# Block attention: scores on 32-row tiles of TensorE, values and softmax sums computed transposed on four column tiles, division there

## The reference, cut to what matters

```
b, s, d = x.shape                       # 16, 128, 128;  H = 16 heads, HD = 8
q, k, v = (split_heads(x @ W) for W in (Wq, Wk, Wv))
scores = einsum('bhqd,bhkd->bhqk', q, k) / sqrt(HD)
attn_w = softmax(scores, axis=-1)
ctx = einsum('bhqk,bhkd->bhqd', attn_w, v)      # back to [b, s, d]
attn_out = ctx @ Wo + bo
out1 = layernorm(x + attn_out, ln1_g, ln1_b)    # the experts read out1
```

## Time and profile before

| | |
|---|---|
| time, median of 3 runs | 1621.97 us (1621.96 to 1628.43) |
| the profiled execution's own time | 1623.44 us |
| its span | 1621.7 us |
| the stage at hand | about 1164 to 1349 us of the span |
| TensorE clock granted, mean | 0.92 of full |

### The profile page before, as it was taken

One profiled execution on the slowest core, in us unless ns is written; L12 is line 12 of the kernel. 1 busy time (PEld: TensorE's weight loads), 2 busy tenths in 40 slices (PEclk: granted clock), 3 DMA queues, 4 the chain that ended last, 5 costly groups with the idle time before them and its releaser, 6 DMA issues. The chain is left out here.

```text
span 1621.7 us, 27487 instructions
## 1 busy us (share of the span) xinstructions
PE 1397.8 (86%) x9061; PEld 1085.9 (67%) x9061; DVE 839.1 (52%) x2258; ACT 728.3 (45%) x1657; POOL 146.7 (9%) x256
## 2 busy tenths in 40 slices
PE   6765689999998789959999997995499996999995
PEld 5631367777777457749999995994377773667664
DVE  4548466666664445445454553345777772122224
ACT  4341466666664311225555553342255551433433
POOL 1010000000000000000000002004233430000000
PEclk9878699999999799969999997996599995999998
DMA  8000000000000000000000001202000000000000
GB/s 323 1 1 0 1 1 2 1 1 1 1 1 1 1 1 1 1 0 1 1 2 1 1 1 43 75 2 104 0 1 1 0 1 0 1 1 1 0 1 26
DMA packets 6429, 24.55 MB, mean 15 GB/s; under 512 B 797, under 2 KB 1311, under 8 KB 5418
## 3 DMA queue, kind: packets, MB, share of 16 engines
q1 hardware_dynamic: 6314, 23.03, 4.1%
HBM read 21.98 MB, written 1.05 MB: 14 GB/s over the span
## 5 line engine op out<-in xcount | busy, mean ns | idle before, releaser
L1304 DVE SCALAR_TENSOR_TENSOR XN<-bank,gate,XN 128x128 f32<-128x128 f32 x256 | 89.9, 351 | 224.7 <-PE bank L1268 222.2
L1284 ACT ACTIVATE e_hidden<-bank,small 128x512 f32<-128x512 f32 x152 | 104.4, 687 | 214.5 <-PE bank L1256 214.5
L765 PE MATMUL bank<-a_va,a_pT 128*128 128x65 f32 x1024 | 130.3, 270 | 0.7 <-ACT a_pT L931 0.6
L1009 DVE TENSOR_REDUCE a_mx<-bank 128x4 f32<-128x512 f32 x128 | 87.8, 686 | 80.2 <-PE bank L805 80.1
L1268 PEld LDWEIGHTS bank<-attention_weights,e_hidden 128*128 128x128 f32 x1024 | 119.2, 192 | 14.8 <-issue 14.8
L765 PEld LDWEIGHTS bank<-a_va,a_pT 128*128 128x128 f32 x1024 | 125.2, 193 | 2.4 <-ACT a_pT L931 1.1
L1256 PE MATMUL bank<-XNT,attention_weights 128*128 128x512 f32 x256 | 121.2, 606 | 1.3 <-PEq L541 1.3
L1268 PE MATMUL bank<-attention_weights,e_hidden 128*128 128x128 f32 x1024 | 119.3, 275 | 0.0
L830 PE MATMUL bank<-attention_weights,a_cv 128*128 128x256 f32 x256 | 84.4, 411 | 15.5 <-issue 15.5
L931 ACT ACTIVATE a_pT<-bank 128x512 f32<-128x512 f32 x128 | 76.1, 595 | 41.9 <-PE bank L839 39.2
L1017 DVE TENSOR_TENSOR a_shifted<-bank,a_mx 128x512 f32<-128x512 f32 x128 | 88.3, 690 | 3.4
(11 more groups left out here) (351 smaller groups left out, 2718.2 us busy)
## 6 DMA issues: line engine op xcount, KB each, us to landing
attention_weights<-in_a SPq DMA_DIRECT2D x2, 2048.0 KB, 11.6
mod_ring<-in_mod_weights SPq DMA_DIRECT2D x4, 576.0 KB
ctx_both<-in_ctx SPq DMA_DIRECT2D x1, 2048.0 KB, 10.1
attention_weights<-in_up SPq DMA_DIRECT2D x1, 2048.0 KB, 7.6
attention_weights<-in_down SPq DMA_DIRECT2D x1, 2048.0 KB, 13.2
down<-in_down SPq DMA_DIRECT2D x1, 1536.0 KB, 18.5
down<-in_mod_weights SPq DMA_DIRECT2D x2, 576.0 KB
X<-in_x SPq DMA_DIRECT2D x4, 256.0 KB, 3.5
```

The costliest lines, as they stand in the source:

```text
L765: last = pe.matmul(value_bank[:, j * (W + 1):(j + 1) * (W + 1)], pT[:, i.slot(2), j * 128:(j + 1) * 128], va[:, p, g // 2 * 8 + 2 * j + g ...
L1009: dve.tensor_reduce(mx[:, i.slot(2), :], score_bank[i.slot(2)][:, :].rearrange("p (h s) -> p h s", h=4), AX.X, ALU.max).then_inc(maxed, 1)
L1284: act.activation(hidden[0:rows, p, f, :], up_bank_of(i, f)[0:rows, :], function, bias=up_bias(g, f)).then_inc(hidden_ready, 1)
L1304: dve.scalar_tensor_tensor(out=total, in0=down_bank[j][:, e * D:(e + 1) * D], scalar=gate_column(k, 4 * q + j, g * per_group + e), in1=tot ...
```

## The change

**Scores.** GpSimd makes one spread block per batch instead of four: `own[row, j]` is 1 where the row's head is head j of its own group, so rows 32r to 32r+31 of `kD` hold the four heads of group r. The scores of group r are then a matmul over those 32 rows only. Two are issued together, in phases 3 and 1, into four score banks instead of two.

**Values.** They are computed transposed, once per batch: `va`, with each head's 8 columns 40 apart among zeros, is the stationary operand, 32 columns at a time; a head's `pT` streams, 128 columns, and the four heads of a group add up in PSUM (j = 0 to 3, each filling its 8 of 32 rows). Group c uses the column tile at 32c. The same with `ones` as the stationary operand gives each sum on the 8 rows of its head. So 32 matmuls of 128 columns stand where 16 of 9 columns did, and `pT` is kept for two whole batches.

**Division and behind it.** VectorE inverts 128 x 128 sums and multiplies once; the result is already `oT`. The transposition L1889 and the copy L1961 are gone. Of the normalisation's tail, VectorE keeps the first step; GpSimd does the two affine steps and the copy (`AFFINE`, a lag of 9 steps). The two side results share the projections' PSUM bank, hence new waits on `added` and `qkv_kept`; `KEEP` has moved behind the subtraction on VectorE, and `OUT` waits for it.

```
...
-    PROJECT, KEEP_QKV, BLOCKS, SCORE, EXP, TURN_P, VALUES, NORM_O, TURN_O, OUT, ADD, NORMALISE, KEEP, TURN_OUT = \
-        0, 1, 4, 3, 5, 5, 6, 6, 7, 7, 7, 8, 9, 10
+    PROJECT, KEEP_QKV, BLOCKS, SCORE, EXP, TURN_P, VALUES, NORM_O, OUT, ADD, NORMALISE, KEEP, TURN_OUT = \
+        0, 1, 2, 3, 5, 5, 6, 6, 7, 7, 8, 10, 10
+    AFFINE = 9
...
+        kD, va = sb("kD", [128, 2, 4, S]), sb("va", [128, 2, H * 40])
+        own, ones = sb("own", [128, 4]), sb("ones", [128, 4 * 40])
...
+        shifted, probs, pT = sb("shifted", [128, 2, 512]), sb("probs", [128, 2, 512]), sb("pT", [128, 2, 4, 512])
...
-        score_bank, turn_bank, value_bank = k.ps[0:2], k.ps[2:4], k.ps[4:6]
-        project_bank, side_bank = k.ps[6], k.ps[7]
...
+        score_bank, turn_bank, value_bank, project_bank = k.ps[0:4], k.ps[4:6], k.ps[6], k.ps[7]
+        turned_out = y_bank = project_bank[:, 384:512]
...
-            pool.memset(va[:, :, :, W:W + 1], 1.0).then_inc(cleared, 1)
+            pool.memset(va[:, :, :], 0.0).then_inc(cleared, 1)
+            pool.memset(ones[:, :], 0.0).then_inc(cleared, 1)
+            pool.wait_ge(cleared, 2)
+            pool.memset(ones[:, :].rearrange("p (j w) -> p j w", w=40)[:, :, 0:W], 1.0).then_inc(cleared, 1)
...
-                if i.alive:
-                    (b, g), p = i.part(4), (i.offset // 4) % 2
-                    await_count(pool, qkv_kept, b + 1)
...
-                    pool.tensor_tensor(kD[:, p, 4 * g:4 * g + 4, :], kT[:, p, :].unsqueeze(1).to_broadcast([128, 4, S]),
-                                       k.hmask[:, 4 * g:4 * g + 4].unsqueeze(2).to_broadcast([128, 4, S]),
-                                       ALU.mult).then_inc(k_spread, 1)
+                if i.alive and i.offset % 4 == 0:
+                    b = batch_of(i)
...
+                    await_count(pool, qkv_kept, n + 1)
...
+                    pool.tensor_tensor(kD[:, p, :, :], kT[:, p, :].unsqueeze(1).to_broadcast([128, 4, S]),
+                                       own[:, :].unsqueeze(2).to_broadcast([128, 4, S]), ALU.mult).then_inc(k_spread, 1)
+                i = at(AFFINE)
...
+                    await_count(pool, scaled_ready, n + 1)
...
+                    pool.tensor_tensor(out[:, p, :], scaled[:, p, :], k.affine3(2), ALU.mult).then_inc(chain, 1)
...
+                    pool.tensor_tensor(out[:, p, :], out[:, p, :], k.affine3(3), ALU.add).then_inc(out_ready, 1)
...
+                    pool.tensor_copy(col(k.out1, n), out[:, p, :]).then_inc(copied, 1)
...
+                    if b.older_than(3):
+                        await_count(pe, added, n - 2)
...
-                if i.alive:
+                if i.alive and i.offset % 2 == 0:
                     m, (b, g), p = i.number, i.part(4), (i.offset // 4) % 2
-                    await_count(pe, k_spread, m + 1)
...
-                        await_count(pe, subtracted, m - 1)
-                    pe.matmul(score_bank[i.slot(2)][:, :], qT[:, p, :],
-                              kD[:, p, 4 * g:4 * g + 4, :].rearrange("p h s -> p (h s)"), start=True,
-                              stop=True).then_inc(scored, 1)
-                i = at(TURN_O)
+                    await_count(pe, k_spread, b + 1)
+                    if i.older_than(4):
+                        await_count(pe, subtracted, m - 2)
+                    for r in (g, g + 1):
+                        rows = slice(32 * r, 32 * r + 32)
+                        pe.matmul(score_bank[r][:, :], qT[rows, p, :],
+                                  kD[rows, p, :, :].rearrange("p h s -> p (h s)"), start=True,
...
-                    await_count(pe, o_normed, b.number + 1)
+                    n, p = b.number, b.slot(2)
...
-                    pe.transpose(side_bank[:, 0:128], on[:, :], k.ident).then_inc(o_turned, 1)
-                i = at(VALUES)
-                if i.alive:
-                    m, (b, g), p = i.number, i.part(4), (i.offset // 4) % 2
...
-                        await_count(pe, o_normed, b - 1)
-                    for j in range(4):
-                        h = 4 * g + j
-                        last = pe.matmul(value_bank[p][:, h * (W + 1):(h + 1) * (W + 1)],
-                                         pT[:, i.slot(2), j * 128:(j + 1) * 128], va[:, p, h, :],
-                                         start=True, stop=True)
-                    last.then_inc(weighted, 1)
+                        await_count(pe, o_normed, n)
+                    else:
...
+                    for at_column, stationary, per_group in ((0, va[:, p, :], 160), (S, ones[:, :], 0)):
+                        for j in range(4):
+                            for c in range(4):
+                                first = c * per_group + 32 * j
+                                last = pe.matmul(value_bank[32 * c:32 * c + 32, at_column:at_column + S],
+                                                 stationary[:, first:first + 32], pT[:, p, c, j * 128:(j + 1) * 128],
+                                                 start=j == 0, stop=j == 3, tile_position=(0, 32 * c))
+                                if at_column and j == 3:
+                                    last.then_inc(weighted, 1)
...
-                    await_count(pe, o_kept, b.number + 1)
-                    pe.matmul(side_bank[:, 128:256], k.ones[0:1, :], k.bias3[0:1, :], start=True, stop=False)
...
+                    await_count(pe, o_normed, b.number + 1)
+                    if b.older_than(1):
+                        await_count(pe, out_kept, b.number)
+                    await_count(pe, qkv_kept, min(b.number + 3, B) if isinstance(b.number, int) else b.number + 3)
...
+                    b = batch_of(i)
+                    await_count(pe, out_ready, b.number + 1)
+                    await_count(pe, qkv_kept, min(b.number + 4, B) if isinstance(b.number, int) else b.number + 4)
+                    pe.transpose(turned_out, out[:, b.slot(2), :], k.ident).then_inc(out_turned, 1)
...
                     m, p = i.number, i.slot(2)
+                    (b, g), q = i.part(4), (i.offset // 4) % 2
                     await_count(act, p_turned, m + 1)
-                    if i.older_than(2):
-                        await_count(act, weighted, m - 1)
-                    act.activation(pT[:, p, :], turn_bank[p][:, :], ACT.Copy).then_inc(p_kept, 1)
+                    if i.older_than(8):
+                        await_count(act, weighted, 4 * b - 4)
+                    act.activation(pT[:, q, g, :], turn_bank[p][:, :], ACT.Copy).then_inc(p_kept, 1)
...
-                    dve.tensor_tensor(out[:, p, :], r1[:, :], k.affine3(3), ALU.add).then_inc(out_ready, 1)
...
-                    dve.tensor_scalar(col(k.out1, n), out[:, p, :], 1.0, None, ALU.mult).then_inc(chain, 1)
...
+                    dve.tensor_scalar(scaled[:, p, :], r1[:, :], stats[:, 6:7], stats[:, 7:8], ALU.subtract,
...
-                    dve.reciprocal(rec[:, :], o[:, :, W:W + 1].rearrange("p h w -> p (h w)")).then_inc(inverted, 1)
+                    dve.reciprocal(rec[:, :], value_bank[:, S:2 * S]).then_inc(inverted, 1)
...
-                        await_count(dve, o_turned, n)
-                    dve.tensor_tensor(on[:, :].rearrange("p (h w) -> p h w", h=H), o[:, :, 0:W],
-                                      rec[:, :].unsqueeze(2).to_broadcast([128, H, W]), ALU.mult).then_inc(o_normed, 1)
+                        await_count(dve, y_done, n)
+                    dve.tensor_tensor(oT[:, :], value_bank[:, 0:S], rec[:, :], ALU.mult).then_inc(o_normed, 1)
...
+                i = at(KEEP)
+                if i.alive and i.offset % 4 == 3:
+                    n = batch_of(i).number
+                    await_count(dve, out_turned, n + 1)
+                    dve.tensor_scalar(col(k.XNT, n), turned_out, 1.0, None, ALU.mult).then_inc(out_kept, 1)
```

More of the change, by code:

```diff
@@ L1857, in body @@
             def body(at):
-                i = at(TURN_OUT)
-                if i.alive and i.offset % 4 == 3:
-                    b = batch_of(i)
-                    await_count(pe, out_ready, b.number + 1)
-                    pe.transpose(side_bank[:, 256:384], out[:, b.slot(2), :], k.ident).then_inc(out_turned, 1)
                 i = at(PROJECT)
@@ L1914, in body @@
                     b = batch_of(i)
-                    await_count(pe, o_kept, b.number + 1)
-                    pe.matmul(side_bank[:, 128:256], k.ones[0:1, :], k.bias3[0:1, :], start=True, stop=False)
-                    pe.matmul(side_bank[:, 128:256], oT[:, :], k.w3[:, 384:512], start=False,
-                              stop=True).then_inc(y_done, 1)
+                    await_count(pe, o_normed, b.number + 1)
+                    if b.older_than(1):
+                        await_count(pe, out_kept, b.number)
+                    await_count(pe, qkv_kept, min(b.number + 3, B) if isinstance(b.number, int) else b.number + 3)
+                    pe.matmul(y_bank, k.ones[0:1, :], k.bias3[0:1, :], start=True, stop=False)
```

(27 more changed lines are left out.)

52 lines of the change are left out of this document (28 added, 24 removed).

## The result

The changed kernel takes 1646.33 us (median of 4 runs, 1639.37 to 1648.37), the kernel before 1621.97 (1617.24 to 1628.43, 4 runs): 1.0137 times, 95% interval 1.0115 to 1.0159. By the medians it is slower by 24 us. The profiled execution took 1645.0 us, against 1623.44.

What follows compares the result with a forecast made beforehand. TensorE bound the kernel before, a loop through all engines would bind after: 15 x (10.45 - 10.66) = -3 us, +3 for the ends, sum 0, so 1622 us relative to the median. Range 1608 to 1651; likeliest case 1612 to 1629.

Steps and rivals of the forecast that it cites:

- The loop through all engines: Block attention stage: waits tying all engines set the period, 10.40 us a batch, taken as 10.45, against 10.66; chance 0.56.
- the six legs: Parts of the loop, values round to values: 1.98, 2.00, 1.75, 1.66, 1.27 and 1.74 us, sum 10.40.
- Column tiles: Values matmuls on TensorE: four column tiles stream fully together, 1.72 us a batch; overlap only in part had chance 0.18.
- the rival at two together (+27): Values: only two column tiles stream together, +27 us, 1649; part of the 0.18 for column tiles in part.
- the mild one (+7): Values: four tiles stream together but lose a fifth, block 2.15 us, +7 us, 1629; chance 0.05.
- the changes of shape: TensorE passing between tile shapes: about 0.2 us each, seven a batch where two were, +1.0 us.
- VectorE: Inversion L2019 grows from 16 to 128 columns: 1.02 us, +0.76; VectorE's own chain 8.1 us a batch, not the bound.
- The ends: Start and end of the stage: +1.5 us for GpSimd's fills, the rest in the last batch; together +3 (0 to +5).
- the sum of 0 for the whole change: Whole kernel: 15 periods give -3 us, the ends +3, so 0; 1622 us relative to the median.
- The clock: Rival: TensorE, idle a quarter of the time, falls to 1.2 GHz; half the batches so +28 us, 1650; chance 0.10.
- the 0.9 that was named as a sign of being wrong: Profile sign: granted clock in the middle of the stage below 0.9 means the prediction is wrong; 1.00 was expected.
- a longer loop: The slower part of the loop case, over 0.5% slower than the kernel before; chance 0.10.

Runs made afterwards that it cites:

- e9: e1 with VectorE's inversion of 128 columns done twice, the first result unread; 1643.68 us.
- e8: e1 with the inversion cut from 128 columns to 16, the division by the other columns' sums left out; 1616.37 us.
- e2: The changed kernel with ScalarE's Ln and Exp of the moments one step later (NORMALISE 8 to 9); 1637.8 us.
- e1: The changed kernel with two useless f32 matmuls of 384 columns a batch on all 128 rows, in TensorE's waits; 1619.57 us.
- e5: e1 with the extra matmuls on 32 rows and 32 columns of TensorE; 1650.65 us.
- e10: e1 with the extra matmuls on all 128 rows and 32 columns of TensorE; 1622.52 us.
- e4: The changed kernel with the scores again as 128-row matmuls and GpSimd spreading k four times; 1649.78 us.
- e7: e3 with one of e1's extra matmuls a batch; 1608.92 us.
- e3: The changed kernel with the moments' Ln and Exp a step later and behind the pT copy, and ScalarE's Exp a step earlier; 1636.36 us.
- e11: e7 with five more matmuls of 512 columns behind the last values of the masked attention, the stage before; 1608.61 us.
- e12: e11 with three more matmuls of 512 columns while VectorE chooses two experts after the stage; 1606.25 us.

## Why the prediction was wrong in its likeliest case

1. **The loop through all engines: right, but not alone.** At full clock the six legs start to start, from the timeline above (predicted in brackets): values to inversion 1294.28 - 1292.12 = 2.16 (1.98); to KEEP 2.06 (2.00); to ADD 1.66 (1.75); to the end of the moments 1.59 (1.66); to the transpositions 1.36 (1.27); to the values 1.63 (1.74). Sum 10.46 (10.40, taken as 10.45). Legs laid end to end always add up to the period; what speaks for the loop is that each has the length forecast, and e9: 0.9 more in it is 0.8 more in the period. What the prediction didn't see are two other ways round that are shorter by less than 0.2 us: one leaves out the inversion (e8), the other the moments (e2). The loop binds, but shortening one of these legs alone wins 0.2 us a batch (e8) or nothing (e2).
2. **Column tiles: right.** The values block takes from 1292.12 to 1294.08, 1.96 us (1.9 forecast), and the next weight load starts at 1294.00. Four column tiles of f32 lose nothing that shows, as the row tiles of the earlier trace rows, and the rival at two together (+27) and the mild one (+7) are out. The pair of scores is 1.13 (1.0), with the changes of shape in it as forecast: TensorE's own 8.3 us against 8.0.
3. **VectorE: right.** L2019 takes 958 ns (1020 forecast); the 6.8 ns a column of the earlier trace rows was a little high.
4. **The ends: right at the start.** From the stage's first memset to the first projection 1.89 us (1169.65 - 1167.76), before 0.51: +1.38 (+1.5). GpSimd's affine steps are 0.456 us each where about 0.3 was taken, hidden but in the last batch. The end wasn't measured apart. With the clock held, the sum of 0 for the whole change measured -2.4 (e1 by the medians), which is 0.2% and well inside what can be told.
5. **The clock: wrong, and it is the whole result.** The step that failed is the rival's "Against: even then TensorE works 8 of 10.4 us, with no long gap", and with it the chance of 0.10. TensorE did work 8.3 of 10.45 us, and the clock averaged 0.88 in the middle, under the 0.9 that was named as a sign of being wrong. The argument looked at idle time alone. I had written in the same rival that tiles leave parts of the array unused, and gave that no weight; e5 and e10 show that the part at work matters here.

The rival's price, "half the batches so is +28: 1650", is near the 1646 measured, and in part by luck. The clock cost 21 us, not 28: a batch two thirds at half clock takes 14.8, 4.2 more than at full clock and not 3.5, but fewer are like that, and up to 6 us of the difference from e1 lie in earlier stages. The stated range of 1608 to 1651 holds 1646 only because it reaches as far as the prices of two rivals. The one that came true had 0.10 of the 0.38 given to slower; the rest stood for column tiles and a longer loop, and neither showed.

What stays open: e5's extra matmuls also change the shape of the tile more often than e10's, so the rows at work, the area at work and the changes between row tiles aren't told apart. e4 speaks for rows or area (no 32-row matmul left, clock 0.95), but TensorE is a little busier in it at full clock (83% against 79%), and the 1-row bias is left. e9 lost the clock with matmuls on all rows in its waits, at 86% busy (9.69 of 11.25 us), where e7, at 89% (115.8 of 130 us), kept it: idle time may count as well. Why the earlier stages take up to 5.6 us more in some executions was not looked into.

The Trainium skill, "TensorE: Matmul & The Clock Gate", section "Measured speedup vs the span model", has 2.38 times for three column tiles. That is not what this case shows for f32: 64 passes of 128 columns at 0.107 would be 6.85 us in turn, and the block took 1.96 with its drain, 3.5 times for four tiles (87% of four; 2.38 is 79% of three).

## What to carry to other kernels

When a change takes work from an engine whose clock is granted by its work, price the time after it at both clocks, and read the granted clock in the profile before anything else: here the whole loss stood in the column PEclk. Where freed TensorE time can't be turned into a shorter period, one useless matmul on all rows in a wait of each batch can pay for itself many times (e7: 0.64 us of it a batch, 27 us less than e3). Then look for the loop: once no engine is full, the period is the way through all of them, and e9's doubling of one leg shows in one run whether that leg is on it. It doesn't show what shortening it would win; for that, shorten it (e8), and in the trace ask of each wait how much later it would have ended by the next way.

## What the runs showed of the hardware that I had not expected

- Useless work made the kernel faster: 1646 to 1620 us, with 32 matmuls of 384 columns in the stage.
- Busy for 91% of the time at full clock, TensorE still lost it (e3). Busy for 83% of a batch at full clock, with the scores on all rows, it mostly kept it (e4, 0.95).
- Extra matmuls of equal length on 128 x 32 kept the clock at 1.00, on 32 x 32 left it at 0.89.
- A clock brought up ahead of a stage (0.81 in place of 0.50) was gone after a wait of 6.4 us for VectorE (e11); one with waits of 1.0 and 0.4 us behind it held for the eight matmuls that followed (e12, 3.7 in place of 6.35 us).
